# POOL's queue issues the loads of w2 for experts 3 to 7 of the first expert layer

## The reference, cut to what matters

```
x = x + 0.5 * ffn(layernorm(x))          # first experts
x = x + attn(layernorm(x))               # middle stage
x = x + 0.5 * ffn(layernorm(x))          # second experts

ffn(x):                                  # 8 experts, capacity 256 tokens each
  probs  = softmax(x @ w_switch + b_switch); routes = argmax(probs)
  pos    = running count of the token within its expert; keep = pos < 256
  buf_e  = the kept tokens, gathered by expert              # 8 x 256 x 256
  h      = relu(buf_e @ w1[e] + b1[e])                      # w1[e]: 256 x 1024
  y      = h @ w2[e] + b2[e]                                # w2[e]: 1024 x 256
  out    = y for a kept token, x for any other
```

## Time and profile before

| | us |
|---|---|
| median of 3 runs | 756.94 (756.48 to 757.34) |
| profiled execution, its own time | 755.68 |
| its span in the trace | 754.0 |

### The profile page before, as it was taken

The page is one execution under the profiler, slowest core; times in us unless marked ns, Lnnn a source line. Parts: engine busy times, 40 slices in busy tenths (PEclk is TensorE's granted clock), DMA queues, the critical chain, the costliest instruction groups (busy, mean ns, idle before and its releaser), DMA issues.

```text
span 754.0 us, 17075 instructions
## 1 busy us (share of the span) xinstructions
PE 670.7 (89%) x6159; PEld 578.7 (77%) x6159; DVE 449.8 (60%) x1243; ACT 401.7 (53%) x809; POOL 317.2 (42%) x462
## 2 busy tenths in 40 slices
PE   7649999984777999999999999999999864999994
PEld 5438999973556788888888888888888753999993
DVE  7853746413477675768777868677665374444330
ACT  5753555512233767676767676767654543544430
POOL 5240573322032443444563654645537454233311
PEclk9759999997899999999999999999999985999997
DMA  8485677403666444534445555544434243466610
GB/s 267 150 267 192 210 253 235 138 30 68 120 102 107 76 84 74 106 70 77 95 85 83 115 91 115 80 91 87 86 64 140 98 100 98 151 199 198 215 59 28
DMA packets 283746, 92.43 MB, mean 123 GB/s; under 512 B 213678, under 2 KB 281381, under 8 KB 283663
## 3 DMA queue, kind: packets, MB, share of 16 engines
q1 hardware_dynamic: 267310, 82.26, 44.9%
q0 software_dynamic: 3840, 8.32, 3.5%
q10 hardware_dynamic: 12512, 0.76, 1.1%
HBM read 61.95 MB, written 29.40 MB: 121 GB/s over the span
## 4 chain that ended last, share of the span: by engine, by line
PE 59%; DMA 4%; DVE 3%; issue 3%; ACT 3%; SPq 2%; POOL 1%; ACTq 1%; POOLq 0%; DVEq 0%
PE bank L1638 53%; PE bank L1650 6%; DMA qkv_rows<-feats 2%; SPq L348 2%; ACTq L354 1%; DMA xb_rows<-late_rows,xb_token 1%; ACT hids L967 1%; POOL hids L742 1%; DMA keys<-qkv_rows 0%; ACT feats L937 0%; ACT ots L990 0%; DMA mid_rows<-xa_fin,xa_slot 0%; DMA x<-mid_rows 0%; DVE zn_ L1556 0%; ACT kvt_ L954 0%
## 5 line engine op out<-in xcount | busy, mean ns | idle before, releaser
L1638 PE MATMUL bank<-down_w,hids 128*128 128x256 f32 x768 | 107.9, 285 | 1.3 <-POOL hids L742 1.3
L742 POOL TENSOR_TENSOR hids<-hid,hids 128x512 fp32r<-128x512 f32 x64 | 83.1, 1298 | 54.5 <-ACT hids L967 54.4
L1638 PE MATMUL bank<-hnts,up_w 128*128 128x512 f32 x384 | 104.5, 407 | 0.0
L1638 PEld LDWEIGHTS bank<-down_w,hids 128*128 128x128 f32 x768 | 97.4, 188 | 4.8 <-POOL hids L742 2.9
L1638 PE MATMUL bank<-qkv_w,xnts 128*128 128x256 f32 (+1 forms) x384 | 80.1, 358 | 9.6 <-DVE xnts L1501 8.7
L1638 PEld LDWEIGHTS bank<-qkv_w,xnts 128*128 128x128 f32 x384 | 63.6, 198 | 21.8 <-DVE xnts L1501 10.5
L1638 PEld LDWEIGHTS bank<-hnts,up_w 128*128 128x128 f32 x384 | 67.5, 189 | 11.5
L964 ACT ACTIVATE hid<-bank,cols 128x512 f32<-128x512 f32 x64 | 44.1, 689 | 47.5 <-PE bank L1638 47.1
L733 POOL TENSOR_SCALAR sth<-sth 128x1 f32<-128x1 f32 x32 | 7.2, 225 | 132.7 <-DVE sth L1513 132.6
L1638 PE MATMUL bank<-a_w,xa_h 128*128 128x256 f32 x256 | 60.1, 379 | 0.0
L1638 PE MATMUL bank<-b_w,xb_h 128*128 128x256 f32 x256 | 60.1, 379 | 0.0
(11 more groups left out here) (273 smaller groups left out, 1446.2 us busy)
## 6 DMA issues: line engine op xcount, KB each, us to landing
qkv_rows<-feats SPq DMA_DIRECT2D x32, 384.0 KB, 3.3
a_raw<-in_L_ffn_w_dram SPq DMA_DIRECT2D x32, 256.0 KB, 4.3
a_w<-in_L_ffn_w_dram SPq DMA_DIRECT2D x32, 256.0 KB, 3.8
b_raw<-in_L_ffn_w_dram SPq DMA_DIRECT2D x32, 256.0 KB, 3.1
b_w<-in_L_ffn_w_dram SPq DMA_DIRECT2D x32, 256.0 KB, 2.8
mid_rows<-x_all SPq DMA_DIRECT2D x8, 512.0 KB, 2.9
x<-mid_rows SPq DMA_DIRECT2D x32, 128.0 KB, 2.6
values<-qkv_rows SPq DMA_DIRECT2D x32, 128.0 KB, 2.8
```

The lines of the kernel that those rows point to most:

```text
L742: pool.tensor_tensor(hids[1][u % 3][:], hid[u % 2][:], f32(hids[0][u % 3][:]), ALU.subtract).then_inc(s_hidl, 1)
L1638: return pe.matmul(dst, left, right, start=start, stop=stop, skip_group_check=True)
```

## The change

For experts 3 to 7 of the first layer the w2 transfer is taken out of SP's `load_weights` and put into POOL's `run_experts`. POOL issues chunk pj of w2[px + 1] in the step of down(px, pj), as the last thing of that step: in the step of chunk 3 it comes behind the two sends, the two gathers and the clearing. It waits until down(px, pj) is done. The 20 transfers have a semaphore of their own per chunk, and PE waits for that. To have these four semaphores, the loads of the middle stage's weights share two instead of four. The second expert layer is as it was.

```diff
+        POOL_LOADS = 3
+
+        def w2_loaded(x, c, ex):
+            if POOL_LOADS <= x < E:
+                return s_w2[c], 16 * (x - POOL_LOADS + 1)
+            return ex.sem.got2[c], 16 * (x + 1 - (E - POOL_LOADS if x >= E else 0))
...
+        def piece_loaded(i):
+            return s_piece[i % 2], 16 * sum(len(pieces[j][2]) for j in range(i % 2, i + 1, 2))
...
                 sp.dma_start(ex.raw[:, :, a:b],
                              w1[x - ex.first, :, a:b].rearrange("(k p) n -> p k n", p=P)).then_inc(ex.sem.got1[c], 16)
+                if POOL_LOADS <= x < E:
+                    return
                 if x >= ex.first + 2:
                     sp.wait_ge(ex.sem.down, (x - 2) * PAIRS + c + 1)
                 sp.dma_start(ex.w2s[x % 2][:, 2 * c:2 * c + 2],
...
+            def load_w2(x, ex, c):
+                a, b = c * 2 * P, (c + 1) * 2 * P
+                pool.wait_ge(ex.sem.down, (x - 1) * PAIRS + c + 1)
+                pool.dma_start(ex.w2s[x % 2][:, 2 * c:2 * c + 2],
+                               w2[x - ex.first, a:b].rearrange("(k p) n -> p k n", p=P)).then_inc(s_w2[c], 16)
...
                                 load_rows(px + 3, ex)
                             if between:
                                 between(px)
+                        if POOL_LOADS <= px + 1 < E:
+                            load_w2(px + 1, ex, pj)
...
-                pe.wait_ge(ex.sem.got2[j], 16 * (x + 1))
+                pe.wait_ge(*w2_loaded(x, j, ex))
```

More of the change, by code:

```diff
@@ L141, in build @@
             sem("a_slots_made"), sem("a_pass_factors"), sem("a_passed"), sem("a_stored"))
-        s_piece = sems("piece_loaded", 4)
+        s_piece = sems("piece_loaded", 2)
         s_shift, s_shifted = sem("last_row_spread"), sem("qkv_rows_shifted")
@@ L154, in build @@
         s_bpos, s_bmark, s_blate, s_bslot = sem("b_places_and_slots"), sem("b_marked"), sem("b_late_factors"), sem("b_slotted")
+        s_w2 = sems("w2_loaded", PAIRS)
         one = {f: sem(f"experts_{f}") for f in ("table", "token", "stat", "root", "unit", "turned", "xt", "xtl",
@@ L480, in load_piece @@
                         sp.wait_ge(s_wlow, chunks_through(i - 2))
-                    sp.dma_start(view[:, :, c:c + n], w.rearrange("(k p) n -> p k n", p=P)).then_inc(s_piece[i], 16)
+                    sp.dma_start(view[:, :, c:c + n], w.rearrange("(k p) n -> p k n", p=P)).then_inc(s_piece[i % 2], 16)
             for u in range(E * PAIRS):
@@ L907, in middle_weights @@
                     else:
-                        act.wait_ge(s_piece[i], 16 * len(pieces[i][2]))
+                        act.wait_ge(*piece_loaded(i))
                     high, given = piece_cut(i, pieces[i][0][0], k, c, False), piece_cut(i, piece_view(i), k, c, True)
@@ L1844, in fold_ln1 @@
                     pe.wait_ge(s_foldq, 4)
-                    pe.wait_ge(s_piece[0], 16 * 3)
+                    pe.wait_ge(*piece_loaded(0))
                     pe.wait_ge(s_shift, 1)
@@ L1857, in _ @@
             run_experts(xa, fold_ln1)
-            pe.wait_ge(s_piece[2], 16)
+            pe.wait_ge(*piece_loaded(2))
             for m in range(KM):
```

## The result

| | before | after |
|---|---|---|
| median of 6 runs, us | 756.71 (755.76 to 759.56) | 761.88 (760.17 to 762.35) |
| ratio of the runs | | 1.006 (95%: 1.004 to 1.008) |
| span of the profiled execution, us | 754.0 | 760.0 |
| its own time, us | 755.68 | 761.75 |

The change makes the kernel 5.2 us slower, 0.7%. Slower was forecast, and the time lies within the range, but the size is little over half of the 9.3 us of the sum.

The account below looks back on a forecast made before the run. PE was taken to bound the first experts, its delay reaching the end one for one. Stall 7.2, clock 1.5 and later experts 0.6 make 9.3 us; on 755.68 plus 1.26 between median and profiled execution, 766 us, range 760.5 to 773.

Parts of the forecast that it names:

- What bounds the kernel: First experts, 60 to 166.8 us: PE is busy throughout, its delay reaches the end; SP's freed queue gives at most 0.04 us.
- Step 1: At expert 4's roots: two w2 issues ahead shift them 2.7 us, and PE waits 0.8 us at the turning.
- Step 2: At down(3,3): chunk 3 of w2[3], issued behind the second clearing, lands late; PE stalls 7.2 us.
- Step 3: In the stall at down(3,3): PE's granted clock falls to 1.2 GHz, and coming back costs 1.5 us.
- Step 4: Experts 4 to 7: later w2 chunks arrive slightly late, 0.6 us of stall in all.
- POOL becomes the bound of the whole stage: Rival, first experts: issues of 2.1 us and landings of 6.4 cost 15.5 us, giving 772.4 us; chance 0.14.
- Cheap issues and fast landings: Rival, at down(3,3): low ends give a 4.3 us stall, 761.2 to 762.7 us in all; chance 0.13.
- Not slower: Rival, at down(3,3): chunk 3 starts ahead of the clearing's end and lands in time, 755.9 to 757.7 us; chance 0.09.

Follow-up runs that it names:

- first_and_late: Changed kernel with w2 transfers ahead of the sends of their step and the clearing after experts 5 and 6 instead of 1 and 2: 754.77 us, ratio 0.9973.
- filled_12: Changed kernel with 12 added PE products, whose results nobody reads, ahead of the wait for w2 at down(3,3): 757.69 us, ratio 1.0012.
- from_expert4: Changed kernel with w2[3] loaded by SP again, POOL issuing 16 transfers for experts 4 to 7: 757.17 us, ratio 1.0013.
- twenty_tiny: Kernel before with 20 added transfers of 8 KB on POOL's queue in the second expert layer, w2 loads staying on SP: 758.16 us, ratio 1.0021.

## Why the prediction was wrong

Its mechanism was right: PE was the only bound of the stage, the lost lead of one transfer made it wait at down(3,3), the clock fell in the wait, and the stage's delay went on to the end. Two terms of the sum were mis-sized, and one was not in it. The stall was forecast half again as long as it was, and the clock too cheap; the stage then cost 6.9 us instead of 9.3, and the drain, which I had not priced, took 2.0 back.

- **What bounds the kernel.** Right. Of the 7.5 us by which the first experts grew in the two traces, 7.2 are PE's wait and its low clock. SP's freed queue is worth nothing, as first_and_late shows: in after fc_w went out 5 us sooner (95.70 against 100.76) and ACT's wait for it is gone, and PE gained nothing by it.
- **Step 1.** Forecast 2.7 us of shift and 0.8 us of wait. The two issues take 1.54 us instead of 2.7; the send moved from 101.75 + 0.88 to 104.42, 1.8 us; PE turned at 102.32, with no wait; the normed rows were ready at 102.26.
- **Step 2, the step that failed.** Forecast 7.2 us, measured 4.8. Of the 2.4 us between, 1.0 is the shift of step 1, 0.2 the gap of 0.30 us which direct transfers don't have, and 1.2 the landing: 3.2 us from 114.00 to 117.20, and 3.4 in the median, where I took 4.4. I had gone by the gathers, as the nearest rows on the same queue. The prediction had the better number in hand: SP's landing for the same transfer (2.9 us) and what POOL's issue is longer, 3.6 by its forecast and 3.3 with the measured 0.78 us. The estimate from the Trainium skill, DMA: Bandwidth & Descriptors, Anatomy of one DMA — SWDGE (gpsimd) path, 3.7 us with the issue, came closer than mine, too. The trace agrees with it: 3.4 less 0.78 of issue is 2.6 us, as that estimate has it.
- **Step 3.** Forecast 1.5 us, measured 2.42, and 2.3 by filled_12. I had taken the price from PE's start at 51.44 and misread it: I set 36 products in one run against three times 12 that each stand behind a down. In the trace the products of that run start 0.213 us apart until the clock is back, 4.4 us after the first, and 0.118 after, which makes the price there 1.9 us and not 1.6. Here PE ran 4.9 us at 1.2 GHz, and two thirds of that were products with w2, which lose more each: they start 0.427 us apart instead of 0.216.
- **Step 4.** Forecast 0.6, measured none: the stall gave POOL time to catch up. That the margins are thin as computed is shown by from_expert4, 1.5 us of wait at down(4,3). The Trainium skill, SBUF — State Buffer, SBUF: two separate sides, had warned of DVE instructions that keep GpSimd from writing descriptors. No such hold-up shows here: the 20 issues lie between 0.71 and 0.83 us, where I had thought of 0.4 us more for each, from the spread of the gathers.
- **Not in the sum.** The drain at the end of POOL's queue, 2.0 us shorter. I had not read the end of the trace, since the change did not touch it. 4.8 + 2.4 - 0.3 - 2.0 = 4.9 us, against 5.2 measured. Without the shorter drain the kernel would stand at about 764 us, nearer to the 766 of the sum.
- **Rivals.** That POOL becomes the bound of the whole stage fell: one issue is 0.78 us. Cheap issues and fast landings gave a stall near the low end (4.3), and 762.7 with the clock: that case was the closer one, and part of its evidence was SP's own row. That its 762.7 lies so near 761.9 is luck: it had 5.8 us for stall and clock, they took 7.2, and the drain took 2.0 away. Not slower happened in first_and_late, where the transfers do start ahead of the clearing, as that rival required; that it was even faster came from the drain, which the rival did not have.

## What to carry to other kernels

A transfer that moves to a queue in strict order inherits the wait of all that stands ahead of it there: give the instant at which it goes out by the longest work ahead (here sends, gathers and 4.2 us of clearing), and compare it with the instant at which it is wanted. Put it ahead of that work; then look for what is now behind the transfers, since an engine without slack meets the next late item at once. Price the landing of a transfer by the row of the same transfer on another queue, and add what the new queue's issue is longer; the row of another transfer on the same queue misled here. And read the last microseconds of the trace, even if the change does not touch them.

## What the runs showed of the hardware

- A wait of 4.6 us on PE cost 7.2 us: 4.8 as such and 2.4 because the granted clock fell to 1.2 GHz before its end and came back 4.9 us after it. Keeping PE busy with products that nobody reads took the second part away (filled_12).
- POOL issues a direct transfer of 256 pieces of 1 KB in 0.78 us (median of 20), one behind the other without a gap, less than an indirect one of 128 pieces (1.06 us and a gap of 0.30).
- The drain behind POOL's last transfer took 6.6 to 10.8 us at the end of these kernels, repeatable to 0.01 us for one kernel, and different with what had been issued on POOL's queue before; the rule is open. It is part of the kernel's time: 20 useless transfers made the kernel 0.3% faster, 20 small ones did not.
- The landing of a gather of 128 rows of 1 KB, counted from its issue, differs between traces of the same code: at most 5.3 us in before and 7.8 in twenty_tiny, where it made PE wait 2.6 us.
